# Columns of x by small loads and 32x32 turns on VectorE, in place of TensorE transposes, from batch 1 on

## The reference

```python
attn_in = tanh(einsum('bsd,da->bsa', x, W1) + b1)          # W1: 512 x 128
scores  = einsum('bsa,a->bs', attn_in, v)
mask    = prefix / postfix / cloze by the batch's prompt type
p       = softmax(where(mask, scores[:, None, :], -1e30))
pooled  = einsum('bjl,bld->bjd', p, x) / count(mask)
h = layernorm(pooled) * gamma + beta
y = silu(h @ dequant(fc1) + fc1_bias)                       # F = 2048
out = x + pooled + 0.5 * (y @ dequant(fc2) + fc2_bias)
```

## Time and profile before

| what | value |
|---|---|
| median of 3 runs | 1659.17 us (1658.46 to 1659.35) |
| profiled execution, its own time | 1657.99 us |
| profiled execution, span | 1656.2 us |
| mean granted TensorE clock | 0.989 |
| PE / PEld busy | 1617.4 / 1308.8 us |
| DVE / ACT / POOL busy | 935.5 / 423.2 / 187.1 us |
| DMA | 52.39 MB, 29679 packets |

### The profile page before, as it was taken

One profiled execution on the slowest core, in us unless ns is written; L12 is line 12 of the kernel. 1 busy time (PEld: TensorE's weight loads), 2 busy tenths in 40 slices (PEclk: granted clock), 3 DMA queues, 4 the chain that ended last, 5 costly groups with the idle time before them and its releaser, 6 DMA issues.

```text
span 1656.2 us, 20819 instructions
## 1 busy us (share of the span) xinstructions
PE 1617.4 (98%) x7648; PEld 1308.8 (79%) x7648; DVE 935.5 (56%) x1827; ACT 423.2 (26%) x632; POOL 187.1 (11%) x140
## 2 busy tenths in 40 slices
PE   4699999999999999999999999999999999999999
PEld 2578878788787878878788787878878788787887
DVE  8887464655646565464664646655465654646612
ACT  2342232322223232232222322232222322223210
POOL 1302011020200102011020100202001020110200
PEclk7799999999999999999999999999999999999999
DMA  9500101010010100101000010100101001010000
GB/s 273 197 1 10 42 1 51 1 51 1 1 52 1 52 1 1 53 0 52 1 28 25 1 51 1 53 1 1 51 1 53 1 1 51 1 52 1 26 0 26
DMA packets 29679, 52.39 MB, mean 32 GB/s; under 512 B 5888, under 2 KB 6400, under 8 KB 29056
## 3 DMA queue, kind: packets, MB, share of 16 engines
q1 hardware_dynamic: 28608, 50.62, 9.2%
q10 hardware_dynamic: 960, 0.27, 0.1%
HBM read 34.10 MB, written 16.78 MB: 31 GB/s over the span
## 4 chain that ended last, share of the span: by engine, by line
PE 95%; DVE 3%; issue 1%; DMA 0%; ACT 0%; SPq 0%; DVEq 0%
PE z_ps L826 14%; PE y_ps L813 14%; PE z_ps L827 14%; PE z_ps L828 14%; PE y_ps L815 14%; PE y_ps L814 14%; PE a_ps L797 2%; PE a_ps L719 2%; PE a_ps L736 1%; PE a_ps L738 1%; PE a_ps L737 1%; PE a_ps L788 1%; PE a_ps L789 1%; PE a_ps L786 1%; PE a_ps L787 1%; PE a_ps L754 1%
## 5 line engine op out<-in xcount | busy, mean ns | idle before, releaser
L826 PE MATMUL z_ps<-w_hi,y_hi 128*128 128x512 f32 x1024 | 413.7, 404 | 0.0
L813 PE MATMUL y_ps<-hT_hi,w_hi 128*128 128x512 f32 x1024 | 403.3, 394 | 3.1 <-DVE hT_lo L629 2.7
L828 PE MATMUL z_ps<-w_hi,y_lo 128*128 128x512 f32 x1024 | 399.7, 390 | 0.0
L815 PE MATMUL y_ps<-hT_hi,w_lo 128*128 128x512 f32 x1024 | 399.6, 390 | 0.0
L827 PE MATMUL z_ps<-w_lo,y_hi 128*128 128x512 f32 x1024 | 399.6, 390 | 0.0
L814 PE MATMUL y_ps<-hT_lo,w_hi 128*128 128x512 f32 x1024 | 399.4, 390 | 0.0
L412 ACT ACTIVATE y_f<-y_ps,b 128x512 f32<-128x512 f32 x256 | 176.6, 690 | 866.7 <-PE y_ps L815 864.6
L652 DVE CAST y_hi<-y_f 128x512 fp32r<-128x512 f32 x256 | 122.0, 477 | 255.1 <-PE z_ps L828 207.7
L826 PEld LDWEIGHTS z_ps<-w_hi,y_hi 128*128 128x128 f32 x1024 | 192.3, 188 | 56.2 <-issue 19.2
L330 POOL TENSOR_TENSOR x<-x,scratch 128x512 f32<-128x512 f32 x64 | 87.6, 1370 | 1250.1 <-ACT scratch L397 1250.1
L813 PEld LDWEIGHTS y_ps<-hT_hi,w_hi 128*128 128x128 f32 x1024 | 192.7, 188 | 44.8 <-issue 3.7
(11 more groups left out here) (142 smaller groups left out, 1146.9 us busy)
## 6 DMA issues: line engine op xcount, KB each, us to landing
x<-in_x_dram SPq DMA_DIRECT2D x64, 256.0 KB, 3.5
out_dram<-x SPq DMA_DIRECT2D x64, 256.0 KB, 2.2
fc_codes<-in_L_ffn_fc_q_dram SPq DMA_DIRECT2D x8, 1024.0 KB, 14.7
fc_scaled<-in_L_ffn_fc_scales_dram SPq DMA_DIRECT2D x8, 1024.0 KB, 16.4
scratch<-in_L_cond_W_dram ACTq DMA_DIRECT2D x1, 256.0 KB, 3.4
b2h<-in_L_ffn_fc_bias_dram SPq DMA_DIRECT2D x1, 256.0 KB, 8.2
tok_i<-in_itok_B_dram ACTq DMA_DIRECT2D x1, 8.0 KB, 5.6
v_col<-in_L_cond_v_dram ACTq DMA_DIRECT2D x1, 0.5 KB, 5.9
```

The costliest lines, as they stand in the source:

```text
L813: mm(o, w1_hi[:, c, cols], hT_hi[:, c, :], start=(c == 0), stop=False)
L815: last = mm(o, w1_lo[:, c, cols], hT_hi[:, c, :], start=False, stop=(c == ND - 1))
L826: mm(z_ps[r][:], y_hi[k % 2][:, rows], w2_hi[:, k, :], start=(k == 0), stop=False)
L828: last = mm(z_ps[r][:], y_lo[k % 2][:, rows], w2_hi[:, k, :], start=False, stop=(k == NF - 1))
```

## The change

From batch 1 on TensorE no longer transposes x. SP loads x a second time, into four buffers x_cols[s] of 128x512 words, by 16 DMAs per batch. Each DMA fills 32 partitions: partition q takes 16 pieces of 32 words (128 bytes), one from each row i*32+q. DVE then turns each x_cols[s] in 32x32 blocks into a slot of `scratch` ("TURN", one instruction per slice), which gives the same slice of the transposed x that TensorE made, now in SBUF. ACT's copy and DVE's subtraction read that slot in place of the PSUM bank, and use two pairs of output buffers in turn (part_hi/part_lo, coef/u_rows) in place of one. The four x_cols buffers share the memory of xs_hi and xs_lo, so the column loads of a batch wait until the batch before has used its last xs block, and stand in SP's order ahead of the stores. At the start they stand between x of batch 1 and weight group 2. The pooling matmul U now waits for x itself, which T did before.

```diff
+        with ExitStack() as early:
+            x_cols = [early.enter_context(nc.sbuf_tensor(f"x_cols{s}", [P, S], F32)) for s in range(ND)]
         xs_hi = [sb(f"xs_hi{i}", [P, D], F32R) for i in range(2)]
...
+        xt_rows = [scratch[:, s * SLOT:s * SLOT + S] for s in range(ND)]
...
-        PE_PLAN = {3: [("T", 0)], 4: [("AT", 0), ("T", 1)], 5: [("AT", 1), ("T", 2)], 6: [("AT", 2), ("T", 3)],
-                   7: [("AT", 3)], 8: [("SC", 0)], 14: [("USUM", 0), ("U", 0)], 16: [("DSUM", 0)],
+        PE_PLAN = {4: [("AT", 0)], 5: [("AT", 1)], 6: [("AT", 2)], 7: [("AT", 3)], 8: [("SC", 0)], 14: [("USUM", 0), ("U", 0)], 16: [("DSUM", 0)],
...
-        DVE_PLAN = {3: [("XT", 0)], 4: [("XT", 1)], 5: [("XT", 2)], 6: [("XT", 3)], 7: [("PAR", 0)],
+        DVE_PLAN = {2: [("TURN", 0)], 3: [("TURN", 1), ("XT", 0)], 4: [("TURN", 2), ("XT", 1)],
+                    5: [("TURN", 3), ("XT", 2)], 6: [("XT", 3)], 7: [("PAR", 0)],
...
-            return a_ps[0][:], part_hi[:], part_lo[:]
+            hi, lo = ((part_hi, part_lo), (coef, u_rows))[s % 2]
+            return xt_rows[s], hi[:], lo[:]
...
+            x_split = x.rearrange("b (i q) d -> b q i d", q=Q)
+
+            def load_columns(a):
+                for s in range(ND):
+                    for j in range(P // Q):
+                        cols = slice(s * P + j * Q, s * P + (j + 1) * Q)
+                        sp.dma_start(x_cols[s][j * Q:(j + 1) * Q, :].rearrange("q (i d) -> q i d", d=Q),
+                                     x_split[bass.ds(a, 1), :, :, cols].rearrange("a q i d -> q (a i) d")).then_inc(cols_in[s], 16)
...
             load_x(1, 1)
+            load_columns(1)
...
             def turn(b, p):
 
+                sp.wait_ge(xs_used, (b + 1) * NJ)
+                load_columns(b + 1)
                 for J in range(NJ):
                     store(b - 1, p, J)
...
             def xt_hi_part(a, s):
-                act.wait_ge(xt_tr, a * NJ + (s + 1))
-                if s >= 1 and not is_first(a):
-                    act.wait_ge(at_done, a * NJ + s)
-                bank, hi, _ = xt_buffers(a, s)
-                copy(hi, bank).then_inc(xt_hi, 1)
+                if is_first(a):
+                    act.wait_ge(xt_tr, s + 1)
+                else:
+                    act.wait_ge(turned, (a - 1) * ND + (s + 1))
+                    if s >= 2:
+                        act.wait_ge(at_done, a * NJ + (s - 1))
+                whole, hi, _ = xt_buffers(a, s)
+                copy(hi, whole).then_inc(xt_hi, 1)
...
+            def turn_columns(a, s, p, ch):
+                if s == 0:
+                    dve.wait_ge(h_tr, a * ND)
+                dve.wait_ge(cols_in[s], a * 64)
+                v.transpose(xt_rows[s], x_cols[s][:]).then_inc(turned, 1)
...
-            def transpose_x(a, s, p):
...
                 for L in range(NJ):
                     rows, place = quadrant(L)
+                    pe.wait_ge(x_in[p][L], a * 8 + (16 - 8 * p))
                     last = mm(a_ps[0][rows, :], e_all[:, L, :], xt[p][:, L, :], start=True, stop=True, **place)
```

More of the change, by code:

```diff
@@ L160, in build @@
         xt_tr = sem("xt_tr")
+        cols_in = [sem(f"cols_in{s}") for s in range(ND)]
+        turned = sem("turned")
         xt_hi = sem("xt_hi")
@@ L520, in __call__ @@
                     self.wait()
+            def turn_columns(a, s, p, ch):
[3 more added lines that the diff above has]
+                v.transpose(xt_rows[s], x_cols[s][:]).then_inc(turned, 1)
             def xt_lo_part(a, s, p, ch):
                 dve.wait_ge(xt_hi, a * NJ + (s + 1))
-                bank, hi, lo = xt_buffers(a, s)
-                v.tensor_tensor(lo, bank, f32(hi), ALU.subtract).then_inc(xt_ready, 1)
+                whole, hi, lo = xt_buffers(a, s)
+                v.tensor_tensor(lo, whole, f32(hi), ALU.subtract).then_inc(xt_ready, 1)
             def split_x(a, n, p, ch):
@@ L629, in split_h @@
                 v.tensor_tensor(hT_lo[:, c, :], f, f32(hT_hi[:, c, :]), ALU.subtract).then_inc(hT_done, 1)
-            steps = {"XT": xt_lo_part, "PAR": params, "SCAN": scans, "COLS": columns, "ROWMAX": row_max,
+            steps = {"TURN": turn_columns, "XT": xt_lo_part, "PAR": params, "SCAN": scans, "COLS": columns, "ROWMAX": row_max,
                      "ARGS": exp_args, "PC": split_pc, "USUM": move_usum, "DSUM": row_scale,
@@ L798, in transpose_h @@
                 last.then_inc(h_tr, 1)
-            steps = {"T": transpose_x, "AT": project, "SC": scores, "U": u_sum, "USUM": e_sums, "DSUM": p_sums,
+            steps = {"AT": project, "SC": scores, "U": u_sum, "USUM": e_sums, "DSUM": p_sums,
                      "PZ": pool_block}
```

## The result

The changed kernel takes 1633.92 us (median of 4 runs, 1632.80 to 1635.25) against 1659.05 us before: a ratio of 0.9849, 95% interval 0.9837 to 0.9862. In a second comparison it took 1633.47 us, ratio 0.9845 (0.9831 to 0.9858). The forecast was 1633.7 us.

The account below looks back on a forecast made before the run. TensorE, busy 98% of the span and 95% of the chain, was taken as the bound. Profiled 1657.99 - 26.7 (transposes) + 1.2 (first overlap) = 1632.5 us; the median lies 1.18 higher, so 1633.7 us; range 1627 to 1645.

Parts of the forecast that it names:

- What is removed: TensorE, 14 ordinary batches: four transpose groups of 0.48 us gone per batch, 1.91 us each, 26.7 us in all.
- best case: Whole kernel: all 60 transpose groups gone at 0.49 us and no loss in the first overlap, 1630.5 us.
- What is added on DVE: DVE, each batch: four turns of 0.6 us (bounds 0.49 and 1.23), 2.4 us per batch, hidden in ordinary batches.
- The sum by the Trainium skill's figure: DVE turns: 311 ns per 128x128 bf16 turn, 1.24 us per slice; the sum is that with the upper bound.
- ffn(0): First overlap, where dequantising makes DVE late: batch 1 gains nothing and costs 1.2 us.
- the sign: First overlap, if right: TensorE's first projection of x waits longer for DVE, about 2.3 us.
- The loads: DMA queues: 8192 pieces of 128 B, 7.2 to 13.6 us per batch, hidden, nothing on the path.
- a sign of being wrong: SP's queue: stores later than the final rows would say that issuing 16 DMAs is slow; no size given.
- the room of 36 to 47 us: Column loads after the last use of xs: first turn due 36 us later; last slice's deadline allows 47.4 us.
- small gain: Rival, chance 0.09: slow matmuls after transposes stay and a turn takes 1.23 us; 16.1 us gained, 1643.1 us.
- dearer pieces: Rival, chance 0.08: 32-partition DMA pieces cost 53 ns, weight group 2 late, 1637.9 us; at 85.6 ns, 1654.6 us.
- The slower case: Rival, chance 0.09: 32-partition DMAs use four of 16 engines, turns late every batch, about 1762 us.

Follow-up runs that it names:

- the first experiment: Changed kernel with TensorE's four groups of transposes of x put back at their old places, result read by nobody: 1660.8 us, ratio to before 1.0008.

## Why the prediction was right

**What is removed.** 26.7 us over 14 batches was said, and 26.7 us is what the 14 batches are shorter. The unread transposes returned all of it, 1403.5 us again, so the reading of the price from starts (0.48 us for a group, with the slow matmuls behind it) is shown, not only argued. One slip in the prediction changes nothing: its best case takes 28.7 us for 60 groups "at 0.49 us", which is 60 groups at 0.48.

**What is added on DVE.** A turn was put at 0.6 us within 0.49 and 1.23; it takes 0.70 us alone, 1.30 us for a pair and 2.48 us for a row of four, so 0.62 to 0.70 us each. The sum by the Trainium skill's figure (VectorE: DVE Perf Modes, The three transpose paths) would have had 1.24 us for a slice, as an estimate; the measurement is near half of it. In an ordinary batch it is free, at this length and doubled. The worked times of the chain were near: XT 0 done at 278.3 by the forecast, at 278.5 in the trace; XT 2 at 285.4, and at 285.1.

**ffn(0).** The loss was forecast at 1.2 us and is 1.3 us in the stretch from the first fc2 to the scores. AT 0 waits 2.21 us, where about 2.3 was given as the sign. The profiled execution lost another microsecond earlier: its first fc2 matmul starts at 70.41 us, against 69.40 before the change. The windows show the granted clock at 0.56 of full speed from 64 to 66 us:

```profile
64.00:66.00 2.00, 2.00 (x6) 1.57 (x6) 0.84 (x2) 0.69 (x1) 0.00 (x0) 0.56 1.04 392
```

and at 1.00 before the change:

```profile
64.00:66.00 2.00, 2.00 (x11) 1.65 (x9) 1.09 (x2) 0.69 (x1) 0.00 (x0) 1.00 0.55 221
```

The second profile of the same changed kernel has 1.00 in that stretch, and its first fc2 matmul starts at 69.42 us:

```profile
64.00:66.00 2.00, 2.00 (x10) 1.66 (x9) 1.07 (x2) 0.69 (x1) 0.00 (x0) 1.00 1.03 389
```

so this microsecond varies from run to run and isn't the change's. With it the spans agree: 26.7 us gained, 1.3 and 1.0 lost, and the difference of the spans, 1656.2 - 1631.8, is 24.4 us.

**The last few tenths.** That forecast and median agree to 0.2 us is in part luck. The profiled execution took 1633.65 us of its own time, 1.15 over the forecast of 1632.5, and the median lay only 0.27 us over it, where 1.18 had been added; the two errors cancel. In the second comparison the two terms were 1632.26 and 1.21 us, both near the forecast. Single runs spread by about 3 us.

**The loads.** 12.7 ns a piece lies just under the stated bounds of 14.1 to 26.5, whose lower one was misread: small pieces alone take 11.3 ns. The DMA engines are busy for 6.7 us (0.558 x 12), and SP's issue takes longer, 8.29 us for 16 DMAs, 0.52 us each. The prediction had named a slow issue as a sign of being wrong, but had not counted it as a term. It mattered for nothing, as the room of 36 to 47 us holds it four times over: 35.3 us of issue is free, 70.6 us is not. At the start the scales of weight group 2 landed 6.3 us later than before, where 7.2 to 13.6 us had been worked out, and 18 us ahead of DVE's use, so this too was hidden as said.

**The rivals.** The small gain fell by the first experiment; dearer pieces by 12.7 ns, where that rival needed 45 ns and more. The slower case rested on DMAs over 32 partitions keeping four of 16 engines busy. Four engines could make a share of at most 25%; the share was 55.8%.

## What to carry to other kernels

Where one engine makes 95% of the chain, price what you take from it by the distance between starts, and include the slower instructions just behind it: here that was 0.48 us for a group in place of the 0.35 us between the first transpose and the next matmul. Work that moves to an idle engine is free only where that engine idles, so go through the stretch that is unlike the others (here the first overlap with its dequantising) by itself, and place the work there by hand. Give a small-piece load a deadline and count its issue as well as its bytes.

## What the runs showed of the hardware

A 128x512 float32 turn in 32x32 blocks takes VectorE 0.62 to 0.71 us. A DMA of 512 pieces costs SP about 0.52 us (64 in 35.33 us: 0.55) whether the pieces are 128, 32 or 16 B, so that the number of DMAs, not bytes, sets the time of such a load: 1 MB took 8.3, 35.3 and 70.6 us. At the start, among the weight loads, it was 1.1 us (16 in 17.56). And matmuls behind a group of 128x128 float32 transposes are slower for a step, by 0.13 us in all, with or without anyone who reads the result.
